# The local attention's exponential read from PSUM with the negated maximum as its bias, one instruction a head

## The chip, the cores and the metric

The kernel runs on one core of one Trainium2 chip. The metric is the device time of one execution in microseconds (us); lower is better. Three runs of the kernel before took 3838.45, 3840.28 and 3841.61 us; the median is 3840.28 us.

The engines are named as in the profile: PE is TensorE's matrix multiplication and PEld its loading of weights, DVE is VectorE, ACT is ScalarE, POOL is GpSimd, SP is SyncE, which issues the DMAs. PSUM has eight banks of 128 x 512 float32.

## The reference, cut to what matters

The program is a small two-stage network over 16 batches of 512 tokens with 128 features. In its first stage a gated recurrence (256 states) is gated by a two-layer transformer with local attention; in its second, an attention over all tokens (16 heads) is gated by experts. The change is in the local attention, which both layers have, with 8 heads of 64 and windows of 64 tokens:

```python
sim = jnp.einsum('bhwid,bhwjd->bhwij', bq, bk)
...
mask = (i < j) | (i > j + WINDOW) | (j == -1)
sim = jnp.where(mask, -jnp.finfo(sim.dtype).max, sim)
attn = jax.nn.softmax(sim, axis=-1)
out = jnp.einsum('bhwij,bhwjd->bhwid', attn, bv)
```

The softmax is computed as exp(sim - max), and the sum over the keys comes out of the product with the values, whose operand has a column of ones.

## The kernel before, in words

**The flows.** The work of one batch is cut into steps, and the steps belong to flows: `pre` (load and norm), `gru` (the gated recurrence), `attn0` and `attn1` (the local attention of the two layers), `post0` and `post1` (their feed-forward parts), `glob` (the attention over all tokens) and `expert`, which runs once. Four lanes hold them: lane a is attn0, post0, attn1 of batch b; lane s is post1 of batch b-1, gru of b, pre of b+1; lane g is the global attention of batches b-2 and b-1; lane x is the experts.

**What sets the order.** Each engine runs its own fixed sequence, once for each of 18 or so turns of a loop over the batches. The strings of `ORDER` (line 268) say from which lane the next step is taken: "a3g" is one step of lane a, then three of lane g. `merged` (line 281) reads them. Nothing is scheduled at run time. An engine waits on semaphores (`need`, line 314) for the step of another engine that it depends on, and what stands behind a waiting instruction waits too.

**The local attention.** A layer has a projection stage and a score stage. In the projection stage, for each of four tiles of 128 tokens (t = 0 to 3), PE computes q, k and v; ACT copies and squares q and k (L933, L936); DVE sums the squares (L1186) and multiplies by the rotary tables (`rot`: L1196, L1198, L1199); POOL adds the two products (L1385); DVE computes the inverse norms in three short instructions (`rot2`: L1207, L1209, L1211); POOL multiplies by them (L1390); PE turns q and k (`tq`, `tk`: L668) and ACT copies them to `qT` and `kT` (L956).

The score stage has eight units, one for each tile and each half of the heads, u = 2t + par. A unit covers 128 queries of four heads, and its scores fill one PSUM bank, `bank_a`: 128 queries x 4 heads x 128 keys. Its steps are

- `score`: PE writes the mask and the products into bank_a (line 678 on). DVE takes the maximum over the keys of each head (L1216), four columns in `stat`, and subtracts it (L1220), from bank_a into `prob[u % 2]` in SBUF;
- `prob`: ACT takes the exponential of `prob[u % 2]` in place, one instruction of 128 x 512 (L959);
- `pturn`: PE turns the probabilities in bank_b (L699), ACT copies them (L965);
- `pv`: PE multiplies by the values in bank_c; DVE takes the reciprocal of the sums (L1228) and scales (L1230);
- `oturn`, `wo`: every second unit, PE turns the output (L723), ACT copies it (L968), PE multiplies by the output weights, DVE adds to the residual (L1238).

There is one score bank. The next unit's `score` waits for the subtraction of the unit before it (line 674). The first projection of the next batch and the first matmul of `post0` wait for the last unit's subtraction (lines 651 and 740).

**What runs beside it.** The global attention has 64 score products a batch (`sim`, three banks of its own). DVE takes each one's negated maximum (L1292, `nmax`), ACT its exponential from PSUM with that column as bias and with the sum (L1022, followed by an ACTIVATION_READ_ACCUMULATOR), PE multiplies four of them by the scaled values (`av`, in o_bank), DVE takes a reciprocal (L1300) and POOL scales values by it (L1424). The recurrence's steps on DVE are L1134 to L1144 (`in_h`, `in_f`, `in_i`), L1148 to L1154, L1157 and L1158 (`g4`), and L1161, L1163 and L1165 (`g5`, the last one the scan).

## Time and profile before

| | |
|---|---|
| three timed runs | 3838.45, 3840.28, 3841.61 us |
| profiled execution, its own time | 3830.7 us |
| its span, first to last instruction | 3828.9 us |
| PE busy | 3102.7 us, 81% |
| DVE busy | 2714.3 us, 71% |
| ACT busy | 2401.6 us, 63% |
| POOL busy | 933.2 us, 24% |
| mean granted TensorE clock | 0.929 of full speed |

Busy time is the union of an engine's instructions, so neighbours that overlap are not counted twice; the busy time of a group of equal instructions is the sum of their durations. Start to start of two neighbours tells what an instruction costs its engine's queue, the duration tells when its result is there. The steady part repeats with a period of about 218.5 us a batch, so one period can be read for all, and the same place of a neighbouring batch lies 218.4 us away.

### The profile page before, as it was taken

The numbers are of one execution on the slowest core, as the hardware profiler recorded it, in microseconds if no ns is written. First come the engines' busy times: TensorE is split into PE (matmuls) and PEld (weight loads), VectorE is DVE, ScalarE is ACT, GpSimd is POOL, SyncE is SP. The second block draws the span as 40 slices with busy tenths as digits, with TensorE's granted clock in tenths as the row PEclk, the third lists the DMA queues.
The fourth block names the chain that finished last, engine by engine and source line by source line (L and its number), as shares of the span: only waits on it lengthen the run. The fifth ranks groups of instructions, "written<-read, shape, count | busy, mean of one in ns | idle before, by whom it ended". The sixth has DMA issues, their size and how long they took to land.

```text
span 3828.9 us, 55334 instructions
## 1 busy us (share of the span) xinstructions
PE 3102.7 (81%) x19984; PEld 1603.7 (42%) x20144; DVE 2714.3 (71%) x4829; ACT 2401.6 (63%) x5082; POOL 933.2 (24%) x685
## 2 busy tenths in 40 slices
PE   4668787888978787887978888897878789797786
PEld 2444443434444443444444344444444344444241
DVE  3476777868687886868687786868778686868432
ACT  2345666766666675766667676666667676666553
POOL 2021322222122322222132222213232221223100
PEclk7779898999999999999999899999989999999997
DMA  2001000010101001010100101010100101010200
GB/s 68 1 4 46 16 30 32 20 53 16 53 16 50 16 22 47 20 49 20 49 20 26 36 20 53 16 53 16 42 20 20 53 19 50 18 49 13 92 26 11
DMA packets 113451, 122.82 MB, mean 32 GB/s; under 512 B 13427, under 2 KB 86685, under 8 KB 113181
## 3 DMA queue, kind: packets, MB, share of 16 engines
q1 hardware_dynamic: 113180, 119.26, 9.7%
q8 instruction: 164, 2.69, 0.3%
q14 instruction: 107, 0.87, 0.1%
HBM read 64.70 MB, written 54.53 MB: 31 GB/s over the span
## 4 chain that ended last, share of the span: by engine, by line
PE 52%; DVE 26%; ACT 11%; issue 6%; POOL 5%; SPq 1%; DMA 0%; DVEq 0%; POOLq 0%; ACTq 0%
PE pb L573 29%; PE o_bank L573 12%; POOL scratch L1390 4%; DVE nmax L1292 4%; PE s L573 4%; PE pb L668 3%; PE pb L699 2%; DVE stat L1216 2%; ACT ex L1022 2%; DVE scratch L1220 2%; DVE scratch L1196 2%; DVE stat L1186 2%; PE pb L723 2%; DVE side L1158 1%; DVE scratch L1230 1%
## 5 line engine op out<-in xcount | busy, mean ns | idle before, releaser
L1022 ACT ACTIVATE ex<-s,nmax 128x512 f32<-128x512 f32 x1024 | 698.3, 686 | 279.7 <-DVE nmax L1292 257.1
L1292 DVE TENSOR_REDUCE nmax<-s 128x1 f32<-128x512 f32 x1024 | 676.2, 680 | 259.8 <-PE s L573 257.1
L573 PE MATMUL o_bank<-ex,vsc 128*64 128x512 f32 x2048 | 528.2, 638 | 84.6 <-POOL vsc L1424 84.2
L1424 POOL TENSOR_TENSOR vsc<-vrow,rinv 128x256 f32<-128x256 f32 x256 | 157.0, 613 | 1724.2 <-DVE rinv L1300 1724.2
L1385 POOL TENSOR_TENSOR scratch<-scratch 128x1024 f32<-128x1024 f32 x128 | 307.1, 2399 | 564.5 <-DVE scratch L1199 538.5
L573 PE MATMUL s<-qs,ks 96*128 96x512 bf16 x1024 | 345.2, 394 | 82.7 <-ACT ex L1022 82.7
L573 PE MATMUL pb<-wqkv,hsh 128*128 128x512 f32 x768 | 379.1, 622 | 33.8 <-DVE hsh L1179 26.1
L573 PE MATMUL pb<-kT,qT 64*64 64x64 f32 (+1 forms) x6144 | 330.8, 257 | 45.1 <-DVE scratch L1220 12.7
L959 ACT ACTIVATE scratch<-scratch 128x512 f32<-128x512 f32 x256 | 160.7, 628 | 321.1 <-DVE scratch L1220 321.0
L668 PE MATMUL pb<-const,scratch 128*128 128x128 f32 x1024 | 165.3, 308 | 242.2 <-POOL scratch L1390 242.2
L573 PEld LDWEIGHTS pb<-kT,qT 64*64 64x64 f32 x6144 | 282.9, 144 | 98.4 <-issue 98.4
L1390 POOL TENSOR_TENSOR scratch<-scratch,stat 128x1024 f32<-128x1024 f32 x128 | 258.1, 2017 | 191.6 <-DVE stat L1211 191.6
L573 PEld LDWEIGHTS o_bank<-ex,vsc 128*64 128x64 f32 x2048 | 133.3, 141 | 354.5 <-issue 249.2
L1216 DVE TENSOR_REDUCE stat<-pb 128x4 f32<-128x512 f32 x256 | 176.0, 687 | 136.1 <-PE pb L573 134.3
L668 PEld LDWEIGHTS pb<-const,scratch 128*128 128x128 f32 x1024 | 134.0, 160 | 320.0 <-issue 207.1
L573 PEld LDWEIGHTS s<-qs,ks 96*128 96x128 bf16 x1024 | 86.1, 98 | 382.5 <-issue 218.8
L573 PE MATMUL pb<-cent,w 128*128 128x512 f32 (+1 forms) x384 | 198.3, 627 | 42.6 <-ACT mlp_h L979 34.6
L573 PEld LDWEIGHTS pb<-wqkv,hsh 128*128 128x128 f32 x768 | 143.7, 197 | 204.1 <-issue 114.6
L956 ACT ACTIVATE qT<-pb 128x512 f32<-128x512 f32 x128 | 76.5, 598 | 220.1 <-PE pb L668 219.9
L933 ACT ACTIVATE scratch<-pb 128x512 f32<-128x512 f32 x256 | 151.9, 593 | 98.9 <-PE pb L573 97.1
L1022 ACT ACTIVATION_READ_ACCUMULATOR ex<-s,nmax 128x1 f32 x1024 | 208.2, 203 | 0.0
L573 PE MATMUL pb<-vb,scratch 128*64 128x65 f32 (+1 forms) x2176 | 192.8, 234 | 17.6 <-DVE scratch L1230 7.4
(190 smaller groups left out, 6108.9 us busy)
## 6 DMA issues: line engine op xcount, KB each, us to landing
parts_store<-side SPq DMA_DIRECT2D x64, 384.0 KB, 2.6
qs<-parts_store SPq DMA_DIRECT2D x128, 192.0 KB, 2.7
ks<-parts_store SPq DMA_DIRECT2D x128, 192.0 KB, 3.2
parts_store<-side SPq DMA_DIRECT2D x64, 256.0 KB, 2.9
parts_store<-side SPq DMA_DIRECT2D x64, 128.0 KB, 2.7
xin<-in_L_attn_x SPq DMA_DIRECT2D x16, 256.0 KB, 3.6
out<-o1T SPq DMA_DIRECT2D x16, 256.0 KB, 4.3
wqkv<-in_L_ffn_wqkv SPq DMA_DIRECT2D x1, 1536.0 KB
```

Source lines behind the costliest of these rows:

```text
L573: return pe.matmul(o, l, r, start=start, stop=stop, skip_group_check=True)
L668: last = pe.transpose(dst[:, P * r:P * r + P], l_q[:, INNER * k + P * r:INNER * k + P * r + P], ident)
L699: last = pe.transpose(bank_b[:, P * r:P * r + P], prob[u % 2][:, r, :], ident)
L723: last = pe.transpose(bank_b[:, P * r:P * r + P], o_row[:, P * r:P * r + P], ident)
L933: A(l_sq[:, INNER * k:INNER * (k + 1)], src, ACT.Square).then_inc(FA, 1)
L959: A(prob[s[1] % 2], prob[s[1] % 2], ACT.Exp).then_inc(FA, 1)
L1022: A(ex[:, w % 2, j, :], s_bank[(2 * NT + c) % SIMS][:], ACT.Exp, bias=nmax[:, c % 8:c % 8 + 1], accum_out=rsum[:, w % 2, j:j + 1]).then_in ...
L1216: V.tensor_reduce(top, sims, X, ALU.max).then_inc(FV, 1)
L1292: V.tensor_reduce(nmax[:, c % 8:c % 8 + 1], s_bank[(2 * NT + c) % SIMS][:], X, ALU.max, negate=True).then_inc(GV, 1)
L1385: G.tensor_tensor(l_q, l_c, l_s, ALU.add).then_inc(f.sem["pool"], 1)
L1390: G.tensor_tensor(q, q, stat[:, 96:112].unsqueeze(2).broadcast_to([P, 2 * HEADS, DH]), ALU.mult)\
L1424: G.tensor_tensor(vsc[:, w % 2].rearrange("p (m a) d -> p m a d", a=2), vrow[:, m:m + 2, 2 * V1 * p:2 * V1 * (p + 1)].rearrange("p m (a d) ...
```

## The change

DVE's maximum is written negated (`negate=True`), and its subtraction is dropped: the mark `sub` goes, and every wait for it becomes a wait for `prob`. The step `prob` on ACT now reads bank_a and writes `prob[u % 2]`. The bias of an ACT instruction is one value a partition, and the four heads have four maxima, so the exponential is four instructions of 128 x 128, each with its column of `stat`. The wait for the turn of unit u - 2, which frees `prob[u % 2]`, moves from DVE to ACT. Bank_a is now freed by the last of the four exponentials. The strings of ORDER are new for all four engines; a line of PE's stands here for them.

```diff
--- before.py
+++ after.py
@@ -188,7 +188,7 @@
     "rot2": {"dve": ["n1", "n2", "inv"], "pool": ["q"]},
     "tq": {"pe": ["t"], "act": ["t"]},
     "tk": {"pe": ["t"], "act": ["t"]},
-    "score": {"pe": ["s"], "dve": ["max", "sub"]},
+    "score": {"pe": ["s"], "dve": ["max"]},
     "prob": {"act": ["p"]},
     "pturn": {"pe": ["t"], "act": ["t"]},
     "pv": {"pe": ["o"], "dve": ["d", "o"]},
@@ -266,15 +266,14 @@
 ORDER = {
-    "pe": ("ga5g2asag2a4gsg5aga2gas3ag3s2a3gsas3gs3a3g3a2g5a2gagsg2ags3g2a2g3agsa2g2as3asg4ag3asa2ga2ga4xg3x4ga2"
...
+    "pe": ("ga4gag2as2a5gsg5ag2asg2as2ga2s3g2asas3gs2ag2a3g3ag3agags2a2gasga2gag2a2g3a3gas2as2agas2ag3asagxg2xa5"
...
@@ -648,7 +647,7 @@
                     elif t:
                         need(pe, f, "act", b, (kind, 0), "c")
                     elif kind == "q":
-                        need(pe, attn[1], "dve", b - 1, ("score", 2 * NT - 1), "sub")
+                        need(pe, attn[1], "act", b - 1, ("prob", 2 * NT - 1), "p")
                         need(pe, f, "dve", b, ("shift",), "h")
                     else:
                         need(pe, attn[1], "act", b - 1, ("oturn", NT - 1), "t")
@@ -671,7 +670,7 @@
                 elif kind == "score":
                     t, par = s[1] // 2, s[1] % 2
                     if s[1]:
-                        need(pe, f, "dve", b, ("score", s[1] - 1), "sub")
+                        need(pe, f, "act", b, ("prob", s[1] - 1), "p")
                     else:
                         need(pe, f, "act", b, ("tq", NT - 2), "t")
                     need(pe, f, "act", b, ("tk", t), "t")
@@ -737,7 +736,7 @@
                         need(pe, f, "pool", b, ("silu3",), "x")
                     else:
                         if l == 0:
-                            need(pe, attn[0], "dve", b, ("score", 2 * NT - 1), "sub")
+                            need(pe, attn[0], "act", b, ("prob", 2 * NT - 1), "p")
                         elif b == B - 1:
                             need(pe, gru, "act", b, ("out",), "o")
                         else:
@@ -955,8 +954,14 @@
                         dst, src = kT[:, :, WIN + P * t:WIN + P * t + P], bank_b if t < NT - 1 else bank_c
                     A(dst, src.rearrange("p (r n) -> p r n", r=PAIRS), ACT.Copy).then_inc(FA, 1)
                 elif kind == "prob":
-                    need(act, f, "dve", b, ("score", s[1]), "sub")
-                    A(prob[s[1] % 2], prob[s[1] % 2], ACT.Exp).then_inc(FA, 1)
+                    u = s[1]
+                    if u >= 2:
+                        need(act, f, "pe", b, ("pturn", u - 2), "t")
+                    need(act, f, "dve", b, ("score", u), "max")
+                    for r in range(PAIRS):
+                        last = A(prob[u % 2][:, r, :], bank_a[:, P * r:P * r + P], ACT.Exp,
+                                 bias=stat[:, 64 + 4 * (u % 2) + r:65 + 4 * (u % 2) + r])
+                    last.then_inc(FA, 1)
                 elif kind == "pturn":
                     u = s[1]
                     need(act, f, "pe", b, s, "t")
@@ -1213,11 +1218,7 @@
                     u = s[1]
                     need(dve, f, "pe", b, s, "s")
                     sims, top = bank_a.rearrange("p (h n) -> p h n", n=P), stat[:, 64 + 4 * (u % 2):68 + 4 * (u % 2)]
-                    V.tensor_reduce(top, sims, X, ALU.max).then_inc(FV, 1)
-                    if u >= 2:
-                        need(dve, f, "pe", b, ("pturn", u - 2), "t")
-                    need(dve, f, "dve", b, s, "max")
-                    V.tensor_tensor(prob[u % 2], sims, top.unsqueeze(2).broadcast_to([P, PAIRS, P]), ALU.subtract).then_inc(FV, 1)
+                    V.tensor_reduce(top, sims, X, ALU.max, negate=True).then_inc(FV, 1)
                 elif kind == "pv":
                     t, par = s[1] // 2, s[1] % 2
                     need(dve, f, "pe", b, s, "o")
```

The order of DVE in the second layer, from the end of the last tile's rotary products to unit 1's maximum. L1157 and L1158 are `g4`, L1161, L1163 and L1165 are `g5`, L1216 and L1220 the score unit's maximum and subtraction, L1207 to L1211 `rot2`. Before:

```order
L1199 TENSOR_TENSOR scratch<-scratch,tab 128x16x32
L1157 TENSOR_TENSOR side<-side 128x512
L1158 TENSOR_TENSOR side<-side 128x512
L1292 TENSOR_REDUCE nmax<-s 128x1
L1216 TENSOR_REDUCE stat<-pb 128x4
L1220 TENSOR_TENSOR scratch<-pb,stat 128x512
L1207 TENSOR_TENSOR stat<-stat 128x16
L1209 TENSOR_TENSOR stat<-stat 128x16
L1211 SCALAR_TENSOR_TENSOR stat<-stat 128x16
L1161 TENSOR_TENSOR side<-side 128x512
```

After, where L1204 is the old L1199, L1293 the old L1292, L1221 the old L1216, L1212 to L1216 the old L1207 to L1211, and L1162, L1163 and L1166 the old L1157, L1158 and L1161:

```order
L1204 TENSOR_TENSOR scratch<-scratch,tab 128x16x32
L1293 TENSOR_REDUCE nmax<-s 128x1 x3
L1301 RECIPROCAL rinv<-rsum 128x4
L1293 TENSOR_REDUCE nmax<-s 128x1
L1221 TENSOR_REDUCE stat<-pb 128x4
L1212 TENSOR_TENSOR stat<-stat 128x16
L1214 TENSOR_TENSOR stat<-stat 128x16
L1216 SCALAR_TENSOR_TENSOR stat<-stat 128x16
L1293 TENSOR_REDUCE nmax<-s 128x1
L1162 TENSOR_TENSOR side<-side 128x512
L1163 TENSOR_TENSOR side<-side 128x512
L1166 TENSOR_TENSOR side<-side 128x512
```

`g4` has moved from in front of the three short instructions to behind them, together with `g5`, and maxima of the global attention have moved in front.

The order of PE at the same place, from the end of unit 0's scores to the start of unit 1's. L668 is the turn of q and k of the last tile, `s<-qs,ks` a global score product, `pb<-masks,identb` the start of a unit's scores. Before:

```order
L573 MATMUL pb<-kT,qT 64x128
L573 MATMUL s<-qs,ks 128x512
L668 MATMUL pb<-const,scratch 128x128 x8
L573 MATMUL pb<-masks,identb 128x512
L573 MATMUL pb<-kT,qT 64x64 x2
```

After, with every line number one lower:

```order
L572 MATMUL pb<-kT,qT 64x128
L572 MATMUL s<-qs,ks 128x512 x2
L572 MATMUL o_bank<-ex,vsc 64x512 x4
L572 MATMUL s<-qs,ks 128x512 x3
L667 MATMUL pb<-const,scratch 128x128 x8
L572 MATMUL s<-qs,ks 128x512
L572 MATMUL pb<-xn,gru_w 128x512
L572 MATMUL pb<-masks,identb 128x512
```

Five global score products and a value product now stand in front of the turn instead of one score product, and one more and a recurrence input behind it.

## Rows read from the trace of the kernel before

**Rows 1.** The core: its span and mean granted clock.

```profile
core 0: 3828.9 us, clock 0.929
```

**Rows 2.** One period: us; busy PE, PEld, DVE, ACT, POOL; granted clock; DMA share; GB/s.

```profile
1610.50:1829.00 218.50, 183.02 (x1228) 94.19 (x1237) 167.53 (x298) 147.05 (x315) 58.24 (x43) 0.96 0.10 32
```

**Rows 3.** First layer's score stage, second layer's projections, second layer's burst.

```profile
1837.00:1885.00 48.00, 46.30 (x431) 27.22 (x434) 32.11 (x63) 30.36 (x68) 6.02 (x8) 1.00 0.10 34
1936.00:1947.00 11.00, 7.47 (x23) 2.36 (x22) 9.43 (x15) 9.40 (x20) 6.55 (x5) 0.84 0.06 23
1961.50:1991.30 29.80, 26.65 (x304) 17.63 (x309) 23.36 (x44) 17.25 (x35) 4.96 (x5) 0.94 0.05 15
```

**Rows 4.** The page: the chain that ended last, by engine.

```profile
PE 52%; DVE 26%; ACT 11%; issue 6%; POOL 5%; SPq 1%; DMA 0%; DVEq 0%; POOLq 0%; ACTq 0%
```

**Rows 5.** Groups by line and shape: busy us, mean ns | idle before, releaser.

```profile
L1022 ACT ACTIVATE ex<-s,nmax 128x512 f32<-128x512 f32 x1024 | 698.3, 686 | 279.7 <-DVE nmax L1292 257.1 <-DVE rinv L1300 22.1
L1220 DVE TENSOR_TENSOR scratch<-pb,stat 128x512 f32<-128x512 f32 x256 | 177.1, 692 | 22.1
L959 ACT ACTIVATE scratch<-scratch 128x512 f32<-128x512 f32 x256 | 160.7, 628 | 321.1 <-DVE scratch L1220 321.0
```

**Rows 6.** Timeline, first layer's score units: start us, us, engine, line [idle before].

```profile
1842.47 0.69 DVE L1216 TENSOR_REDUCE stat<-pb 128x4 f32<-128x512 f32 x1
1845.62 0.68 DVE L1216 TENSOR_REDUCE stat<-pb 128x4 f32<-128x512 f32 x1
1846.41 0.69 DVE L1220 TENSOR_TENSOR scratch<-pb,stat 128x512 f32<-128x512 f32 x1
...
1848.69 0.69 DVE L1216 TENSOR_REDUCE stat<-pb 128x4 f32<-128x512 f32 x1 [0.39 <-PE pb L573]
...
1847.13 0.63 ACT L959 ACTIVATE scratch<-scratch 128x512 f32<-128x512 f32 x1 [1.35 <-DVE scratch L1220]
```

**Rows 7.** Timeline of ACT: instructions that follow each other without a wait.

```profile
1921.36 0.69 ACT L1022 ACTIVATE ex<-s,nmax 128x512 f32<-128x512 f32 x1
1921.93 0.21 ACT L1022 ACTIVATION_READ_ACCUMULATOR ex<-s,nmax 128x1 f32 x1
...
1927.21 0.22 ACT L946 ACTIVATE stat<-stat 128x16 f32<-128x16 f32 x1
1927.46 0.31 ACT L948 ACTIVATE stat<-stat,cols 128x16 f32<-128x16 f32 x1
1927.67 0.58 ACT L933 ACTIVATE scratch<-pb 128x512 f32<-128x512 f32 x1
```

**Rows 8.** Timeline of DVE, POOL and PE at the second layer's hinge.

```profile
1948.82 0.68 DVE L1157 TENSOR_TENSOR side<-side 128x512 f32<-128x512 f32 x1
1949.42 2.83 DVE L1158 TENSOR_TENSOR side<-side 128x512 f32<-128x512 f32 x1
1952.17 0.68 DVE L1292 TENSOR_REDUCE nmax<-s 128x1 f32<-128x512 f32 x1
...
1955.31 2.27 DVE L1163 TENSOR_TENSOR side<-side 128x512 f32<-128x512 f32 x1
...
1948.98 2.72 POOL L1385 TENSOR_TENSOR scratch<-scratch 128x1024 f32<-128x1024 f32 x1 [2.90 <-DVE scratch L1199]
1954.81 2.22 POOL L1390 TENSOR_TENSOR scratch<-scratch,stat 128x1024 f32<-128x1024 f32 x1 [3.12 <-DVE stat L1211]
...
1957.17 1.94 PE L668 MATMUL pb<-const,scratch 128*128 128x128 f32 x8 [7.12 <-POOL scratch L1390]
```

**Rows 9.** Timeline of DVE in the second layer's burst.

```profile
1961.54 0.69 DVE L1216 TENSOR_REDUCE stat<-pb 128x4 f32<-128x512 f32 x1 [1.12 <-PE pb L573]
...
1986.64 0.68 DVE L1158 TENSOR_TENSOR side<-side 128x512 f32<-128x512 f32 x1
...
1991.22 0.68 DVE L1216 TENSOR_REDUCE stat<-pb 128x4 f32<-128x512 f32 x1
```

**Rows 10.** The stretch of the lower clock; columns as in the second group.

```profile
1951.50:1965.20 13.70, 7.67 (x48) 5.47 (x51) 10.93 (x16) 3.61 (x7) 2.42 (x2) 0.50 0.00 0
```

More of the change, by code:

```diff
@@ L268 @@
 ORDER = {
[L269 to L277 removed]
+    "pe": ("ga4gag2as2a5gsg5ag2asg2as2ga2s3g2asas3gs2ag2a3g3ag3agags2a2gasga2gag2a2g3a3gas2as2agas2ag3asagxg2xa5"
+           "x2gxagx3gxg4a2g2a2gagxgs6asgs4g5a4g5xagaxax2a3g2axa4gxg4xg2x2ags5as2as11aga2g2ag3asxg2as2gaxs16xg3xg"
+           "xa11xsag5xa3ga"),
+    "act": ("2ga3g4agagsa2gs4as2g4as3ags2g2s4a6g3asaga2g2asg2ag2agsga2s4gagagagagasg2s2asg2a2sa2sa2gxg2a6g4a4g3ag"
+            "3a2g4a3gx3ag2agags2a2gs3a3gxgasg3ag9a2gs2as2asa2g2agsg3xagsagsg2x2gx2sagx2g"),
+    "dve": ("a3gsx3gag2agsgaga3g2a2sa2gagagasgsgasa4g2sags2g2a2gas2ags2ga2gsg2aga3gas2gasags2a2sasg2a2s2as4x3ag3a"
+            "3g2ags2g2as2agsa4g2as2g2a3gxs3x2a5g2ag2sagsg2asasas4as2g2a4xsgas3a5g16xas2gaga5xg2sgxgax"),
+    "pool": ("2g3ag2ag3a2g2s5g3agasag2agsa2s3g"),
 }
```

8 lines of the change are left out of this document (removed).

## The prediction

> **What bounds the kernel now.** The core's span is 3828.9 us [rows 1]; the profiled execution took 3830.7 us, 1.8 us around the span, and the three timed runs have a median of 3840.28 us, 9.6 us above it. I make the sum against 3830.7 and add the 9.6 at the end.
>
> I read the busy time by stretch first. The program repeats once a batch, and a period of 218.5 us has PE busy for 183 us, DVE 168, ACT 147 and POOL 58 [rows 2]. None is full, so I asked where each one is. In the first layer's eight score units (48 us) PE is busy for 46.3 us: this stage is PE's. In the second layer's burst, from the max of unit 1 to the max of unit 7 (29.8 us), PE has 26.65 and DVE 23.36: two engines take turns. In 11 us of that layer's projections, shortly ahead of the burst, PE has only 7.5 while DVE has 9.4 [rows 3]. The chain that ended last says the same over the whole run: PE 52%, DVE 26%, ACT 11% [rows 4]. So DVE time is worth something in the second layer and little in the first.
>
> **The change part by part. 1, DVE.** There are 256 score units (2 layers, 8 units, 16 batches). Each loses the subtraction L1220, 692 ns long [rows 5], and the wait for its own max: the max starts at 1845.62, the subtraction at 1846.41, the next max can start at 1848.69 [rows 6]. From the max's start to the end of the subtraction that is 0.79 + 0.69 = 1.48 us of DVE's queue; a max alone takes 0.69. Neighbours overlap by some 0.1 us, so I count 0.70 us saved a unit, 11.2 us of the 168 in a period.
>
> **2, ACT.** One exponential of 128x512 without a bias column (L959, 628 ns [rows 5]) becomes four of 128x128 from PSUM with one. The trace of before has no such shape, so I bound it. The global attention's exponential, 128x512 from PSUM with a bias column, takes 686 ns [rows 5] and its follower starts 0.57 us after it; one of 16 columns from SBUF with a bias column (L948) takes 0.31 us and its follower starts 0.21 to 0.22 us after it [rows 7]. The slope between a 16-column and a 512-column instruction is (628 - 220) / 496 = 0.83 ns a column (L946 takes 0.22 us for 16 columns [rows 7], L959 628 ns for 512). So 128 columns from PSUM: 686 - 384 x 0.83 = 366 ns, follower after 570 - 320 = 250 ns. From SBUF: 0.31 + 112 x 0.83 ns = 0.40 us, follower after 0.31 us. Four then last 3 x 0.25 + 0.37 = 1.12 us, at most 3 x 0.31 + 0.40 = 1.33. If the bias were free while columns count alone, it would be the 0.63 of now. I take 1.12, the row with the same source and the same kind of bias. ACT's queue holds 1.0 us a unit instead of 0.52, 7.7 us more a period on an engine that has 147 of 218.5.
>
> The Trainium skill, ScalarE: Activation LUTs, section What ACT_TABLE_LOAD costs, gives 280 ns + 0.833 ns a column for an instruction with a pointer bias and 93 ns of overlap between neighbours. As an estimate by that page four take 3 x 294 + 387 = 1.27 us, 0.15 us a unit more than by my row; on the at most eight tight handovers counted below that would add 1.2 us a period.
>
> **3, the score bank is held longer.** Now bank_a is free when the subtraction ends, 1.48 us after the max starts [rows 6]. After the change it is free when the fourth exponential ends: max 0.69, 0.03 to ACT (the subtraction ends at 1847.10, L959 starts at 1847.13 [rows 6]), then 1.12: 1.84 us. So a tight handover is 0.36 us later (0.57 by the upper bound; below nothing if the exponentials took 0.63). The tight cadence is 3.07 us now, 1845.62 to 1848.69 [rows 6], and becomes 3.43. The probabilities themselves are ready sooner: 0.79 + 0.69 + 0.03 + 0.63 = 2.14 us after the max now, 1.84 then.
>
> In the first layer PE is the bound and PE's work there is unchanged. Two of its handovers are tight, 3.15 us from 1842.47 and 3.07 from 1845.62 [rows 6], so I charge 2 x 0.36 = 0.7 us a period, with nothing gained.
>
> **4, the new order at the second layer's hinge.** This is where I expect most. Now PE stands idle for 7.12 us before the last turn of q (L668, 1957.17), until POOL's L1390 that starts at 1954.81. L1390 waits for DVE, which first does L1157 and L1158 of the gated recurrence (from 1948.82; L1158 alone takes 2.83 us beside POOL's L1385, against 0.68 where POOL is idle, 1986.64), one global max, the max and the subtraction of unit 0, and only then the three short instructions [rows 8, 9]. In the new order L1157 and L1158 stand behind those three, and two global maxima come in front. From the end of L1199 to the three: minus 3.35 us (1948.82 to 1952.17, where the global max starts), minus 0.70 for the subtraction, plus 2 x 0.6 for the maxima, plus 0.1 for a reciprocal: 2.75 us earlier, so the turn of q starts at 1954.4 instead of 1957.2. PE gets five score products and one value product of the global attention in front of that turn (0.3 to 0.4 each and 1.9 us), so the 7.1 us of idleness nearly fill up. But unit 1's max now has L1157 to L1165 in front of it. After the three at 1951.8 stand one global max, 0.6, and a recurrence of 0.6 + 2.8 + 0.7 + 0.7 + 1.3 (its L1163 took 2.27 beside POOL [rows 8] and should now miss it): the earliest max of unit 1 is 1958.5. On PE's side it waits for the turns, a recurrence input and a score, 4.4 + 1.9 us at today's pace: 1960.7. Now it is 1961.54 [rows 9]. The gain lies between 0.8 and 3 us; I take 1.5.
>
> **5, the burst behind it.** From unit 1's max to unit 7's it is 29.7 us now (1961.54 to 1991.22 [rows 9]). Of PE's work 1.9 us of value product and four score products of 0.35 have moved ahead: 3.3 us. Of DVE's, six subtractions (4.2 us) and three maxima (1.8) are gone and two recurrence inputs (1.3) come in: 4.7 us. The longer hold costs between nothing and 6 x 0.36 = 2.2; other work of PE stands between most pairs of scores, so I take 0.8. With the smaller of the two gains that is 3.3 - 0.8 = 2.5 us. If every handover is bound by the bank, the floor is 6 x 3.43 = 20.6 us, still below PE's 23.
>
> **Sum:** +0.7 - 1.5 - 2.5 = -3.3 us a period, 16 periods: -53 us. 3830.7 - 53 + 9.6 = 3787 us. Its own range, from the bounds of parts 4 and 5 (-2 to -5 a period): 3760 to 3808.
>
> **Rivals.**
> A, the clock comes back as well. For the 13.7 us from 1951.5 the granted clock is 0.50, the lower level (1.2 GHz) [rows 10], and this follows PE's idleness at the hinge. If the fill of part 4 keeps it at 2.4 GHz, the 7.67 us of PE work in that window [rows 10] halve: 3.8 us more a period, -7.1 in all, 3726 us. For it: the fill stands exactly in the gap. Against it: PE would still wait for the turns, and DVE holds unit 1 back.
>
> B, slower: the exponentials come late in ACT's queue, and the bank with them. Today a late exponential holds nothing but its own transposition, since the bank is DVE's to free. Place: the seven handovers of the first layer, where PE has 1.7 us of slack in 48 [rows 3]. Price: one global exponential ahead on ACT, 0.57 us, and the 0.36, 0.93 x 7 = 6.5 us, less the 4.0 of the second layer: +2.5 a period, 3840 + 40 = 3880 us. It decides from 4.0 / 7 = 0.57 us a handover, that is, once the exponentials start 0.21 us late on average. For it: ACT starts L959 0.03 us behind DVE only where it is idle [rows 6]. Against it: ACT has 147 of 218.5.
>
> C, no change: another loop through PE sets the period. PE's 183 us a period are not touched by any edit, and what the second layer gains is waited away in front of the next stage: 3840 us.
>
> **Chances.** Forecast 0.44, A 0.18, B 0.25, C 0.13. A measurement of this kernel tells 0.2%, some 8 us, from no change. Faster 0.62, same 0.13, slower 0.25. The range leaves out the outer half of B and little of A: 3722 to 3868 us.
>
> **What would show it.** Right: DVE busy for 157 us a period, ACT for about 155; the four exponentials 0.25 us apart and 0.37 long; the wait before the last turn of q in the second layer under 4 us; unit 1 to unit 7 in 26 to 28 us; the first layer's 48 us within 1 us. A: no half clock in the burst. B: PE's waits for the exponentials sum to over 5 us a period in the first layer. Wrong in part 2: an exponential over 0.40 us. The forecast falls if the first layer grows by more than the second one gives back, or if a longer half clock appears.

## The result, and the profile after

The changed kernel takes 3906.98 us (3904.78 to 3908.12, four runs) against 3839.36 us before: the ratio is 1.0176, 95% interval [1.0159, 1.0194]. It is slower by 68 us, 4.2 us a period; the forecast was 53 us faster. The profiled execution has this core:

```profile
core 0: 3904.8 us, clock 0.920
```

The period seen from one first maximum of the first layer to the next, in four stages: the first layer's units 0 to 7; from its last maximum to unit 1's in the second layer; the second layer's burst (unit 1 to 7); and the rest. Columns as in [rows 2]. Before:

```profile
1831.10:1871.40 40.30, 38.39 (x373) 22.59 (x378) 32.71 (x65) 28.62 (x67) 7.99 (x9) 1.00 0.05 15
1871.40:1961.50 90.10, 69.13 (x306) 32.31 (x307) 62.94 (x100) 53.54 (x108) 26.09 (x16) 0.93 0.16 54
1961.50:1991.20 29.70, 26.55 (x303) 17.53 (x308) 23.27 (x43) 17.25 (x35) 4.96 (x5) 0.94 0.05 15
1991.20:2049.40 58.20, 48.87 (x249) 21.72 (x249) 48.45 (x90) 47.42 (x105) 19.04 (x13) 1.00 0.06 19
```

After: the period, then the same four stages, and the burst of a later batch.

```profile
1883.10:2108.40 225.30, 192.46 (x1237) 97.53 (x1238) 157.20 (x282) 155.35 (x362) 57.31 (x42) 0.94 0.10 31
1883.10:1924.70 41.60, 38.96 (x375) 22.18 (x376) 28.19 (x58) 30.91 (x84) 8.53 (x9) 1.00 0.04 11
1924.70:2015.50 90.80, 73.68 (x321) 32.79 (x320) 59.96 (x102) 57.94 (x123) 25.39 (x16) 0.94 0.17 55
2015.50:2049.70 34.20, 29.92 (x294) 20.49 (x295) 19.69 (x35) 17.92 (x46) 4.38 (x4) 0.75 0.05 13
2049.70:2108.40 58.70, 49.90 (x250) 22.07 (x251) 49.35 (x90) 48.58 (x109) 19.01 (x13) 1.00 0.07 19
...
2691.50:2721.00 29.50, 24.41 (x294) 17.15 (x295) 19.13 (x35) 17.92 (x46) 4.38 (x4) 0.94 0.05 14
```

This period is 225.3 us against 218.3: +1.3 in the first layer, +0.7 up to unit 1, +4.5 in the burst, +0.5 behind it. DVE and ACT, at 157.20 and 155.35 us, are busy just as forecast ([rows 2] had 168 and 147). The burst shows two things. At a mean clock of 0.75 it takes 34.2 us; two of eleven batches, with the clock that [rows 3] had (0.94), take 29.5 and 30.0. So at the old clock nothing is gained where 2.5 us were forecast, and in the other nine the lower clock adds 4.7. (Averaged over batches 4 to 14, counted from 0, the period is 219.7 us before and 224.3 after, since two of before's take 224.4 with 37.5 us at half clock.)

The chain that ended last, for [rows 4], has passed from DVE to ACT:

```profile
PE 53%; DVE 20%; ACT 17%; issue 5%; POOL 4%; SPq 1%; DMA 0%; POOLq 0%; DVEq 0%; ACTq 0%
```

The groups and one tight handover in the first layer, for [rows 5] and [rows 6]:

```profile
L962 ACT ACTIVATE scratch<-pb,stat 128x128 f32<-128x128 f32 x1024 | 291.9, 370 | 329.1 <-DVE stat L1221 321.8
```

```profile
1895.53 0.69 DVE L1221 TENSOR_REDUCE stat<-pb 128x4 f32<-128x512 f32 x1 [0.17 <-PE pb L572]
...
1896.32 1.14 ACT L962 ACTIVATE scratch<-pb,stat 128x128 f32<-128x128 f32 x4
...
1897.51 0.39 PE L572 MATMUL pb<-masks,identb 128*128 128x512 bf16 x1 [0.49 <-ACT scratch L962]
```

Each exponential lasts 0.37 us, four take 1.14, and the next starts (1.14 - 0.37) / 3 = 0.26 us behind the last: the 0.37, 1.12 and 0.25 of part 2. The next scores start 1.98 us after the maximum. Before they could start 1.53 us after it, when their weights were loaded behind the subtraction (the maximum of [rows 6] starts at 1845.62):

```profile
1847.15 0.10 PEld L573 LDWEIGHTS pb<-masks,identb 128*128 128x128 bf16 x1 [0.57 <-DVE scratch L1220]
```

So a handover is 0.45 us longer where 0.36 were forecast; most of the missing 0.09 is ACT's start, 0.79 us after the maximum's start instead of 0.72.

The hinge, for [rows 8]: PE, POOL, DVE and ACT.

```profile
1997.73 1.12 PE L572 MATMUL o_bank<-ex,vsc 128*64 128x512 f32 x2 [4.22 <-POOL vsc L1425]
...
2007.25 1.94 PE L572 MATMUL o_bank<-ex,vsc 128*64 128x512 f32 x8 [1.41 <-POOL vsc L1425]
...
2011.15 1.06 PE L667 MATMUL pb<-const,scratch 128*128 128x128 f32 x8 [1.21 <-POOL scratch L1391]
...
1995.98 1.60 POOL L1425 TENSOR_TENSOR vsc<-vrow,rinv 128x256 f32<-128x256 f32 x1
...
2003.70 2.35 POOL L1386 TENSOR_TENSOR scratch<-scratch 128x1024 f32<-128x1024 f32 x1 [3.02 <-PE pb L667]
...
2002.36 0.68 DVE L1204 TENSOR_TENSOR scratch<-scratch,tab 128x512 f32<-128x512 f32 x1
...
2005.66 0.69 DVE L1293 TENSOR_REDUCE nmax<-s 128x1 f32<-128x512 f32 x1 [1.43 <-PE s L572]
...
2008.38 0.17 DVE L1212 TENSOR_TENSOR stat<-stat 128x16 f32<-128x16 f32 x1 [0.76 <-ACT stat L947]
...
2007.79 0.21 ACT L945 ACTIVATE stat<-stat 128x16 f32<-128x16 f32 x1
```

The 7.12 us before the turn of q are now 1.21, but 4.22 and 1.41 us stand in front of two value products: 6.84 us in all. The first of these two products stood at the same place before and waited there too, 2.17 us, so that its wait grew by 2.05:

```profile
1940.75 3.21 PE L573 MATMUL o_bank<-ex,vsc 128*64 128x512 f32 x8 [2.17 <-POOL vsc L1424]
```

In the changed kernel it waits for POOL's L1425, which stands behind a rotary sum and then takes 1.60 us. And the three short instructions of DVE come no sooner after the last rotary product than they did: 6.02 us (2002.36 to 2008.38), against 5.88 before (1948.21 to 1954.09). DVE waits there 1.43 us for a score product that PE has not issued and 0.76 us for ACT's L947, which in the new order stands behind four global exponentials.

Unit 1's scores then wait another 0.69 us for unit 0's exponentials. These start 5.86 us after their maximum (2006.93), behind ACT's two copies of the turned q and k:

```profile
2012.79 1.15 ACT L962 ACTIVATE scratch<-pb,stat 128x128 f32<-128x128 f32 x4
...
2013.99 0.39 PE L572 MATMUL pb<-masks,identb 128*128 128x512 bf16 x1 [0.69 <-ACT scratch L962]
```

PE's waits in the burst at the clock of 0.94 (us in total, times, longest), before (1961.5 to 1991.2) and after (2691.5 to 2721.0):

```profile
PE pb L573 <- DVE scratch L1220: 0.4, 1, 0.4
PE pb L723 <- ACT scratch L965: 0.2, 1, 0.2
```

```profile
PE pb L572 <- ACT scratch L962: 2.2, 2, 1.4
...
PE pb L722 <- ACT scratch L970: 1.3, 1, 1.3
```

PE's work there fell from 26.55 to 24.41 us, its idle time rose from 29.7 - 26.55 = 3.15 to 29.5 - 24.41 = 5.09. The bank costs 1.8 us more, and the copy of the turned probabilities (L970, the old L965), which now stands behind four exponentials on ACT, 1.1 more; a wait for DVE's scaling grew by 0.6, and small ones of 1.0 in all are gone.

The same sums over the whole run, before and then after:

```profile
PE pb L668 <- POOL scratch L1390: 242.2, 98, 8.1
PE o_bank L573 <- POOL vsc L1424: 84.2, 61, 6.0
PE s L573 <- ACT ex L1022: 82.7, 73, 2.5
...
PE pb L573 <- DVE scratch L1220: 20.6, 36, 1.2
```

```profile
PE o_bank L572 <- POOL vsc L1425: 153.0, 89, 4.5
PE s L572 <- ACT ex L1027: 108.4, 91, 2.5
PE pb L667 <- POOL scratch L1391: 81.7, 83, 7.0
PE pb L572 <- ACT scratch L962: 60.9, 72, 1.8
```

The hinge's own wait lost 160 us; the value products' got 69 back, the global scores' 26 and the score bank's 40 (60.9 for 20.6).

### The profile page after: what moved, and what is told of

The parts are those of the page before. It is cut to its first block, busy times and chain, and to the rows that moved or that the text cites. A ratio compares the mean times of both kernels' runs of the same rounds, so it can differ in the third digit from the quotient of the medians.

```text
span 3904.8 us, 56006 instructions
## 1 busy us (share of the span) xinstructions
PE 3220.5 (82%) x20144; PEld 1637.3 (42%) x20144; DVE 2544.2 (65%) x4573; ACT 2536.7 (65%) x5850; POOL 922.2 (24%) x685
## 4 chain that ended last, share of the span: by engine, by line
PE 53%; DVE 20%; ACT 17%; issue 5%; POOL 4%; SPq 1%; DMA 0%; POOLq 0%; DVEq 0%; ACTq 0%
PE pb L572 32%; PE o_bank L572 12%; ACT ex L1027 4%; PE s L572 3%; ACT scratch L962 3%; PE pb L698 3%; DVE nmax L1293 3%; DVE scratch L1201 2%; DVE stat L1191 2%; POOL scratch L1391 2%; DVE stat L1221 1%; PE pb L667 1%; POOL vsc L1425 1%; PE pb L722 1%; POOL scratch L1386 1%
## 5 line engine op out<-in xcount | busy, mean ns | idle before, releaser
L1293 DVE TENSOR_REDUCE nmax<-s 128x1 f32<-128x512 f32 x1024 | 676.6, 679 | 320.0 <-PE s L572 317.2
L572 PE MATMUL o_bank<-ex,vsc 128*64 128x512 f32 x2048 | 546.0, 657 | 155.2 <-POOL vsc L1425 153.0
L1425 POOL TENSOR_TENSOR vsc<-vrow,rinv 128x256 f32<-128x256 f32 x256 | 171.5, 670 | 1623.2 <-DVE rinv L1301 1623.1
L962 ACT ACTIVATE scratch<-pb,stat 128x128 f32<-128x128 f32 x1024 | 291.9, 370 | 329.1 <-DVE stat L1221 321.8
L572 PE MATMUL pb<-wqkv,hsh 128*128 128x512 f32 x768 | 378.2, 624 | 35.0 <-DVE hsh L1184 27.5
L572 PE MATMUL pb<-kT,qT 64*64 64x64 f32 (+1 forms) x6144 | 346.1, 265 | 0.0
L572 PEld LDWEIGHTS pb<-kT,qT 64*64 64x64 f32 x6144 | 296.8, 150 | 93.2 <-issue 93.2
L1221 DVE TENSOR_REDUCE stat<-pb 128x4 f32<-128x512 f32 x256 | 176.5, 690 | 216.3 <-PE pb L572 215.0
L932 ACT ACTIVATE scratch<-pb 128x512 f32<-128x512 f32 x256 | 152.4, 595 | 100.7 <-PE pb L572 100.6
L667 PE MATMUL pb<-const,scratch 128*128 128x128 f32 x1024 | 149.3, 290 | 81.7 <-POOL scratch L1391 81.7
L572 PE MATMUL pb<-vb,scratch 128*64 128x65 f32 (+1 forms) x2176 | 205.7, 243 | 9.9 <-DVE x L1239 6.5
L973 ACT ACTIVATE scratch<-pb 128x512 f32<-128x512 f32 x128 | 76.8, 600 | 209.9 <-PE pb L722 209.9
L572 PEld LDWEIGHTS pb<-vb,scratch 128*64 128x64 f32 (+1 forms) x2176 | 170.4, 152 | 95.0 <-issue 52.2
```

The source lines that it names most:

```text
L572: return pe.matmul(o, l, r, start=start, stop=stop, skip_group_check=True)
L667: last = pe.transpose(dst[:, P * r:P * r + P], l_q[:, INNER * k + P * r:INNER * k + P * r + P], ident)
L932: A(l_sq[:, INNER * k:INNER * (k + 1)], src, ACT.Square).then_inc(FA, 1)
L962: last = A(prob[u % 2][:, r, :], bank_a[:, P * r:P * r + P], ACT.Exp, bias=stat[:, 64 + 4 * (u % 2) + r:65 + 4 * (u % 2) + r])
L1221: V.tensor_reduce(top, sims, X, ALU.max, negate=True).then_inc(FV, 1)
L1293: V.tensor_reduce(nmax[:, c % 8:c % 8 + 1], s_bank[(2 * NT + c) % SIMS][:], X, ALU.max, negate=True).then_inc(GV, 1)
```

## The experiments

Times are medians, and the ratio is to the kernel before on the same chip (3837 to 3839.5 us), with its 95% interval. Stage lengths and half-clock times are means over batches 4 to 14, from maximum to maximum. The clock's price stands apart in a few places: for each kernel I added up PE's busy time inside the stretches of the lower clock (1.2 GHz for 2.4) and halved it, and call what is left of the period the rest. It takes PE to be the bound in those stretches, so it is an upper bound.

| kernel | period | clock | rest |
|---|---|---|---|
| before | 219.7 | 7.3 | 212.4 |
| after | 224.3 | 11.1 | 213.2 |
| old order, four exponentials | 239.2 | 18.3 | 221.0 |
| old order, hold alone | 236.7 | 16.3 | 220.4 |
| new order, first head's maximum | 215.7 | 3.9 | 211.8 |
| the same, ACT's queue filled | 218.5 | 7.1 | 211.4 |
| new order, joint maximum | 216.9 | 6.1 | 210.8 |

**1. The two halves of the change apart.** The body of after with the order of before, and the reverse.

```diff
 ORDER = {...}          # e1_exp_old_order: after.py with the four strings of before.py
 ORDER = {...}          # e2_new_order_only: before.py with the four strings of after.py
```

> The changed exponential with the ORDER strings of the kernel before. Clock theory (the loss of about 67 us comes from the lower clock in the second layer's burst, which the new order brings about by taking PE's filler out of the burst): the granted clock keeps the pattern of before, about 17 us at the lower level a period, and the time is 3835 to 3860 us. Hold theory (the loss comes from the score bank, held about 0.44 us longer at each tight handover, whatever the order): 3880 to 3920 us, with handovers of 1.97 us after the max.

> The kernel before with the ORDER strings of the changed one; DVE's subtraction and the single exponential stay. Clock theory in its form that the order alone removes the filler: 3870 to 3920 us, with 25 us or more at the lower clock a period. Hold theory: the order is harmless and its shorter hinge pays, 3800 to 3845 us.

Measured: 4115.77 us, 1.0730 [1.0701, 1.0759], and 3909.98 us, 1.0192 [1.0166, 1.0217]. The four corners:

| | order of before | order of after |
|---|---|---|
| subtraction on DVE | 3837 | 3910 |
| four exponentials from the bank | 4116 | 3907 |

They don't add up. In the old order the exponentials cost 279 us; the new order alone costs 73, and within it the body is worth nothing (-3, which the intervals don't tell from 0). So the order is needed by the new body and is dear by itself.

**2. The longer hold alone.** DVE still subtracts, but the next scores wait for the exponential.

```diff
-                        need(pe, f, "dve", b, ("score", s[1] - 1), "sub")
+                        need(pe, f, "act", b, ("prob", s[1] - 1), "p")
```

> The kernel before, with one wait changed: the next unit's scores wait for the exponential instead of the subtraction, so the bank is held some 0.65 us longer and nothing else moves. Hold theory: with about 8 tight handovers a period that is at least 4 to 5 us a period, 3905 to 3925 us. Clock theory: only where the extra gap tips the clock is it more than 2 us a period; without a tip 3845 to 3875 us.

> The new order with the subtraction kept and the bank freed by the exponential (the longer hold alone, in the new order; the same edit in the old order cost 248 us). If the new order was laid out for the exponential to free the bank (ACT's exponentials start early in it): 3925 to 3990 us. If the hold costs the same in any order: 4130 to 4170 us.

Measured: 4085.03 us, 1.0651 [1.0626, 1.0675], in the old order; 3937.97 us, 1.0284 [1.0246, 1.0321], in the new one. One wait moved costs 248 us in the old order and 28 in the new. So most of the old order's loss comes when ACT and not DVE releases the bank, already with one exponential a unit: PE's waits for the bank are 156.5 us with the moved wait and 159.8 in the kernel of the first experiment, against 20.6 before, and the first layer's 40.3 us became 50.8 and 55.5.

```profile
PE pb L573 <- ACT scratch L959: 156.5, 107, 2.6
```

```profile
PE pb L573 <- ACT scratch L963: 159.8, 93, 3.1
```

**3. One exponential instead of four.** The first head's maximum serves as bias for all four heads.

```diff
-                    for r in range(PAIRS):
-                        last = A(prob[u % 2][:, r, :], bank_a[:, P * r:P * r + P], ACT.Exp,
-                                 bias=stat[:, 64 + 4 * (u % 2) + r:65 + 4 * (u % 2) + r])
-                    last.then_inc(FA, 1)
+                    A(prob[u % 2], bank_a.rearrange("p (h n) -> p h n", n=P), ACT.Exp,
+                      bias=stat[:, 64 + 4 * (u % 2):65 + 4 * (u % 2)]).then_inc(FA, 1)
```

> The changed exponential as one instruction of 128x512 with one head's maximum as the bias of all four heads (the other three heads' probabilities are therefore wrong), in the order of before. The bank is held 0.72 + 0.69 = 1.41 us, less than the 1.54 of before, and DVE loses its subtraction. Hold theory: faster than before by 1 to 3 us a period, 3790 to 3825 us. Clock theory: the pattern of the clock as before or better, 3780 to 3840 us. If it is no faster than before, DVE's subtraction was worth nothing in that order.

> The changed kernel in its own order, with the exponential as one instruction of 128x512 whose bias is one head's maximum (the other three heads' probabilities are wrong). ACT's queue is relieved by 0.4 us a unit and the bank is free 0.4 us sooner after the max. Handover theory (the burst of the second layer is set by the chain score, max, exponential, next score, so DVE's and PE's relief is worth nothing): 4 to 5 handovers a layer shorten by 0.4 us, 3 to 4 us a period, 3845 to 3865 us. If the chain is not in the handovers: 3890 to 3910 us.

(Both texts call the other three heads' probabilities wrong. That was mistaken: a row's exponentials and their sum carry the same factor, whatever was subtracted, and the division takes it out as long as nothing overflows.)

Measured: 4001.95 us, 1.0432 [1.0408, 1.0457], in the old order; 3767.09 us, 0.9799 [0.9766, 0.9833], in the new one. In the old order both theories had a time near or below that of before, and both missed: although DVE has lost its subtraction, the kernel is 165 us slower than before, and PE still waits 131.3 us for the bank, with 50.2 us for the first layer. The split adds 114 us there.

```profile
PE pb L573 <- ACT scratch L962: 131.3, 94, 2.7
```

In the new order the split into four costs 140 us. Read from the kernel with the new order and the old body (3910), dropping the subtraction and taking the exponential from the bank is worth 143 us, and the split takes 140 of them back. By the table the split's 8.6 us a period are 7.2 of clock and 1.4 of rest, and the rest is nearly the first layer's 1.2 (41.5 us against 40.3).

**4. The bank or ACT's queue?** One exponential, and behind it, when the bank has been let go, two of one column that keep ACT busy.

```diff
+                    for i in range(2):
+                        c = 52 + 4 * l + 2 * (u % 2) + i
+                        A(cols[:, c:c + 1], norm_bias, ACT.Exp, bias=norm_bias)
```

> The kernel with one exponential 128x512 per unit in the changed order (3767 us, the first head's maximum serves all four), and behind each exponential, after it has let the bank go, a wait that is long met and two exponentials of one column into cells that nobody reads: some 0.22 us each, so that ScalarE is occupied about as long per unit as with the four exponentials (1.12 against 0.69 us), while the bank is released as early as with one. Theory 'the longer hold of the bank is the price of the split': the time stays near the kernel with one exponential, 3767 to 3795 us, and the handover from maximum to next scores stays 0.4 us shorter than in the changed kernel. Rival 'ScalarE's own time is the price' (the copies of the turned probabilities queue behind the exponentials): 3870 to 3905 us, near the changed kernel's 3907.

Measured: 3826.27 us, 0.9972 [0.9960, 0.9985], between the two theories. ACT is held 0.69 us and then 0.47 more:

```profile
1850.55 0.69 ACT L961 ACTIVATE scratch<-pb,stat 128x512 f32<-128x512 f32 x1 [0.34 <-DVE stat L1224]
1851.14 0.47 ACT L967 ACTIVATE cols<-cols 128x1 f32<-128x1 f32 x2
1851.51 0.58 ACT L973 ACTIVATE scratch<-pb 128x512 f32<-128x512 f32 x1
```

ACT's longer queue costs 59 of the 140 us, and neither theory had that. The first layer stays at 40.4 us and a burst without half clock takes 27.9 us instead of 27.5; but half clock falls in more batches (15.5 us a period against 8.7), and in the table the whole difference is clock. The remaining 81 us belong to the longer hold, by subtraction and not by a run of its own.

**5. Why the old order loses so much.** First the four steps `prob` 1, 2, 5 and 6 of the first layer moved forward in ACT's row, because they started up to 5.5 us after their maximum; then, on PE instead, work moved in front of two score units.

```diff
 ACT (e10_early_prob):  prob 1, 2, 5, 6 of attn0 moved ahead of the steps they stood behind
 PE  (e15_pe_moves):   +av.11, sim 12.2, sim 12.3    ahead of attn0's score.1
                       +av.14                        ahead of attn0's score.6
```

> The changed exponential in the order of before, which cost 279 us more than before, with four steps moved in ACT's order of the first layer alone: the exponentials of units 1, 2, 5 and 6 stand earlier, ahead of the gate's silu1 and silu2, of three global exponentials and of the first query projection. Late-exponential theory (rival B of the prediction: in the old order the exponential starts up to 5.5 us after its max, and now it holds the bank): the first layer's score stage falls from 55.7 us by 5 us or more, 3990 to 4050 us. If the length of the hold alone counts, not its start: 4090 us or more.

> The exponentials from the bank in the order of before (4116 us, first layer's units 0 to 7 in 55.5 us), and on TensorE three steps of the first layer's stretch moved: the global attention's value product 11 and two of its score groups ahead of unit 1's scores, value product 14 ahead of unit 6's scores. VectorE's, ScalarE's and GpSimd's orders are those of before. Theory 'the scores stand too early in TensorE's row, and everything behind them waits for the bank': TensorE has work for the 2 to 3 us in which it now stands before units 1 and 6, the stretch falls to 49 to 52 us and the time to 4020 to 4080 us. Rival 'what fails in that order is the other engines' turn, not TensorE's': the moved steps were not late, the stretch stays within 1 us of 55.5 and the time within 15 of 4116.

Measured: 4096.12 us, 1.0653 [1.0609, 1.0696], and 4061.93 us, 1.0583 [1.0560, 1.0605], against 4115.77 unmoved. In the first, the exponentials of those units start 0.79 us or less after their maximum and the first layer still takes 55.1 us. The bank's waits over the run fell from 159.8 to 119.6 us, but the global scores' waits for ACT rose from 79.1 to 105.5: the steps that were passed over came late instead. Late exponentials alone were therefore not what held it; an order of ACT without either delay was not tried. In the second it falls from 55.5 to 50.7 us, PE's waits for the bank from 159.8 to 102.2, and the rest of the period from 221.0 to 215.7. So PE's row is a part of it, 54 of the 279 us: a score unit that stands too early there stops all work behind it. The row before unit 1's scores in the unmoved kernel:

```profile
1979.75 0.61 PE L573 MATMUL pb<-masks,identb 128*128 128x512 bf16 x1 [3.11 <-ACT scratch L963]
```

The other 10 us of that stage are not accounted for by a run, nor is it known which places in the rows make up the rest of the 279.

**6. The hinge in the kernel before.** `g4` (L1157, L1158) moved behind the last `rot2` of the second layer, nothing else; then the same with 12 bf16 matmuls of 128x512 ahead of the turn of q, whose results are overwritten; and 24 of them in the kernel before as it was.

```diff
 DVE:  -L1157, L1158    ahead of L1207, L1209, L1211 (second layer, tile 3)
       +L1157, L1158    behind them
+                    if l and t == NT - 1 and not k:
+                        for _ in range(12):      # 24 in e6_filler_before
+                            mm(dst, identb[:], masks[:, 0, :, :].rearrange("p h n -> p (h n)"))
```

> The kernel before with one move in DVE's order: the recurrence's L1157 and L1158 stand behind the three short instructions of the last tile instead of in front of them, which is the prediction's part 4 alone. The prediction's reasoning: the turn of q starts some 3.3 us earlier and unit 1's max 1 to 3 us earlier, 3790 to 3825 us. If the recurrence then holds unit 1's max back by as much: 3835 to 3850 us.

> The kernel before with the recurrence's L1157 and L1158 moved behind the three short instructions, which gave 3816 us, and 12 bf16 products of the mask as filler in PE's gap of 4 us before the last turn of q in the second layer. In the run without filler the batches alternate between 216 and 221 us with 13.7 and 27.3 us at the lower clock. Clock theory: all batches near 216 us or less, 3770 to 3800 us. If the dips only wander to the next stage, as in the changed kernel with filler: 3805 to 3825 us.

> The kernel before, with 24 bf16 products of the mask in the 7.12 us for which PE stands idle before the last turn of q in the second layer; their results are overwritten. Clock theory: the 13.7 us at the lower clock behind that gap go or shrink, 3 to 4 us a period less, 3775 to 3800 us. If PE's pace in that stretch does not set the time: 3830 to 3850 us.

Measured: 3816.01 us, 0.9948 [0.9933, 0.9964]; 3786.68 us, 0.9847 [0.9805, 0.9889]; and 3829.12 us, 0.9985 [0.9975, 0.9995]. The hinge's move is worth 21 us alone. Its batches come in two kinds: six of eleven take 215.9 to 218.1 us with 13.7 to 23.9 at half clock, and five take 221.0 with 27.3. In the best, unit 1's maximum comes 0.9 us earlier and the burst is 1.5 us shorter (28.2). Filling PE's gap behind the move brings another 29 us, with half clock down from 20.8 to 9.6 us a period (read from its fastest execution, 3773 us; the four go up to 3795). Without the move the filler brings 8 us: half clock falls from 21.4 to 15.5 us, but in seven of eleven batches the turn of q starts 0.7 to 2.0 us later after unit 0's maximum than before.

**7. The clock in the changed kernel.** Fillers of the same kind in the second layer's burst (after: five ahead of unit 2's scores, five and three ahead of the first two output turns and projections; joint maximum: three and three at the first output turn and projection), and one value product moved back behind unit 0's value product.

```diff
+                        if l and s[1] == 2:                      # e5_filler_after, and at two more places
+                            need(pe, f, "act", b, ("tk", NT - 1), "t")
+                            for _ in range(5):
+                                mm(bank_c, identb[:], masks[:, 0, :, :].rearrange("p h n -> p (h n)"))
 PE (e12_av3_back):    -av.3 ahead of attn1's pv.0
                       +av.3 behind it
```

> The changed kernel with idle PE time filled in the second layer's burst: five bf16 products of the mask (0.22 us each at the upper clock) before unit 2's scores, and five and three before the turn of the output and the output product of tiles 0 and 1. Their results are overwritten. Clock theory, in the form left after the first runs (in the new order the lower clock in this burst costs some 6 us a period: batches whose burst runs at the upper level take 219.3 us against 225.3): less than 20 us at the lower clock a period and 3815 to 3875 us. If the clock is only a follower and the waits set the time: 3905 to 3930 us, the filler adding a little.

> The changed kernel with one move in PE's order: the value product of global head 3 (1.9 us) goes back from the gap before the last turn of q into the burst, behind unit 0's value product, where it stood before the change. Clock theory: the burst keeps the upper clock in most batches, 29.5 to 31 us instead of 34.2, 3830 to 3875 us. If the dips come anyway: 3895 to 3920 us.

> The kernel with one joint maximum and one exponential, and in the second layer three matmuls 128x512 in bf16 ahead of the first turn of the attention's output and three ahead of the first output projection, whose results are overwritten: work that keeps TensorE from standing still there, where the granted clock falls in the time after the second layer's burst (8.7 us at half clock per period with one exponential). Theory 'the clock's fall costs there': the half-clock time falls to 4 us or less and 1 to 2 us per period come back, 3735 to 3755 us. Rival 'the fillers cost what they save', as in the changed kernel, where fillers took the half-clock time from 24.5 to 13.7 us and left the time at 3904: 3760 to 3785 us.

Measured: 3903.95 us, 1.0175 [1.0158, 1.0191]; 3922.78 us, 1.0205 [1.0169, 1.0241]; and 3848.99 us, 1.0027 [1.0016, 1.0038], which is 72 us above its own base. In the first, no half clock is left in the burst, which falls from 33.4 to 31.7 us, but the stage behind it grows by 1.7. In the third, six fillers a period make the base worse: its burst, 27.5 us in the base's undisturbed batches, is 31.7 at a clock of 0.89, and the stage ahead of it is 2.4 us longer.

```profile
1885.90:1977.00 91.10, 75.24 (x320) 33.38 (x320) 59.26 (x103) 57.09 (x117) 25.38 (x16) 0.93 0.17 55
1977.00:2008.70 31.70, 25.59 (x295) 18.35 (x301) 19.86 (x35) 15.22 (x28) 5.35 (x4) 0.89 0.04 13
```

In the first the clock's price falls from 11.1 to 6.2 us and the rest rises from 213.2 to 217.4, about the fillers' own time (21 of 0.22 us, 4.6 us); in the third the price rises from 6.1 to 9.1 although PE is busier. In the second, the burst takes 33.8 us and 27.3 us of the period are at half clock. None gained. What the clock costs can be read; where it falls could not be steered by these fillers.

**8. One joint maximum, one exponential.** A softmax row may be shifted by any number, so four heads can share one maximum.

```diff
-                    V.tensor_reduce(top, sims, X, ALU.max, negate=True).then_inc(FV, 1)
+                    V.tensor_reduce(top[:, 0:1], bank_a, X, ALU.max, negate=True).then_inc(FV, 1)
```

with ACT's single instruction of the third experiment.

> The changed kernel with one maximum per unit over all four heads' scores (a reduction 128x512 to 128x1, negated) and one exponential 128x512 with it as bias. A softmax may be shifted by any number, so the four heads may share one maximum; the work per element on VectorE is what it was. Theory 'the split holds the bank': VectorE's reduction of the same 512 columns takes the same 0.72 us as now, the handover from one unit's scores to the next is that of the kernel with one exponential and the first head's maximum, and so is the time, 3767 us, within 10. Rival 'the maximum's result comes sooner or later with one group instead of four': each of 15 handovers moves by 0.1 us, 16 x 1.5 = 24 us, 3743 or 3791 us.

Measured: 3776.76 us, 0.9841 [0.9820, 0.9862]. This version beats both kernels, before by 62 us and the change by 130. No exponential exceeds one; a head whose largest score lies some 87 below the joint maximum would underflow in float32, which is the condition on the data under which it may be used. Its handover and two bursts, of neighbouring batches:

```profile
1814.50 0.68 DVE L1218 TENSOR_REDUCE stat<-pb 128x1 f32<-128x512 f32 x1
...
1815.28 0.69 ACT L961 ACTIVATE scratch<-pb,stat 128x512 f32<-128x512 f32 x1
...
1817.56 0.69 DVE L1218 TENSOR_REDUCE stat<-pb 128x1 f32<-128x512 f32 x1 [0.75 <-PE pb L572]
```

```profile
1931.40:1958.90 27.50, 22.02 (x290) 16.03 (x295) 19.76 (x36) 15.11 (x28) 4.78 (x4) 1.00 0.05 16
...
2146.60:2177.20 30.60, 26.14 (x290) 18.67 (x294) 19.50 (x35) 15.22 (x28) 4.38 (x4) 0.83 0.05 14
```

From maximum to maximum 3.06 us, against 3.52 with four exponentials (1895.53 to 1899.05) and 3.07 before. Six of eleven batches have the slower burst, against two of eleven with the first head's maximum: four times 3.1 us, which is about the 10 us between the two kernels (3767 and 3777).

## Why the prediction was wrong

**Part 1, DVE,** held: 157 us a period. With ACT answering in one instruction, the new body was worth 143 us in the new order.

**Part 2, ACT,** held: 1.14 us for 1.12. The upper bound of 1.33 and the 1.27 estimated by the Trainium skill (ScalarE: Activation LUTs, What ACT_TABLE_LOAD costs) were both too high here.

**Part 3, the hold,** held nearly in size, 0.45 us for 0.36. The first layer grew by 1.3 us where 0.7 were charged: three of its handovers are tight and not two, 1 to 2, 2 to 3 and 5 to 6, each 3.5 us from maximum to maximum, and 0.25, 0.46 and 0.27 us longer than with one exponential.

**Part 4, the hinge, is the first step that failed.** I moved DVE's three short instructions forward by what left DVE's queue in front of them, and took all else as ready. What they need from ACT (L947), and the score products that the maxima in front of them need from PE, had been moved back in those engines' rows, and they came 6.02 us after the rotary product, as before. PE's wait before the turn did shrink, as forecast, but the value product a step earlier waited 4.22 us instead of 2.17, because its scale had queued on DVE and POOL, and a second value product waited 1.41. With the subtraction kept and the new order alone, the same three waits are 4.21, 1.41 and 1.21 us: they come from the order and not from the exponentials. Alone in the order of before, the move of `g4` brought 21 us (experiment 6), near the 16 x 1.5 = 24 forecast, though more of it in the burst than up to unit 1's maximum; so it is the rest of the new order that took it back.

Of the -1.5 us to unit 1's maximum the period above has +0.7. From the first layer's last maximum to it, PE's idle time fell from 90.10 - 69.13 = 20.97 us to 90.80 - 73.68 = 17.12, but its busy time rose by 4.55: the idleness was filled with moved work, and no time came out. The clock explains little of this. One place in this stretch is slower by 1.7 us, six matmuls of `post0` that take 4.44 us in the changed kernel and 2.74 in the one with one exponential, as in the kernel before (at 1907.99):

```profile
1961.69 4.44 PE L572 MATMUL pb<-mlp_h,w 128*128 128x512 f32 x6
```

```profile
1878.18 2.74 PE L572 MATMUL pb<-mlp_h,w 128*128 128x512 f32 x6
```

But over the whole of it half clock lasted 13.5 us before and 10.2 after, and its price, by the upper bound above, is 3.9 and 4.3 us. My 1.5 also leaned on a quicker PE: at the old pace my own figure for PE's side gave 0.8.

**Part 5, the burst, is the term that decides,** and it failed three times over. Of 3.3 us of PE's work that I moved ahead, 2.1 left the burst. For the hold I charged 0.8 us, because other work of PE stands between the scores; it cost 1.8, not because every handover was tight but because two were very tight (1.4 and 0.8 us of waiting). And I charged nothing for what queues behind the exponentials on ACT, PE's 1.1 us for the copy of the turned probabilities: I had called the longer ACT queue 7.7 us on an engine with 147 of 218.5, that is, by its share and not by who waits behind it. Together -2.1 and +1.9: nothing gained at the clock of [rows 3]. Then the clock, of which the sum had nothing: 17.1 us of the burst are at the lower level ((1 - 0.75) x 2 x 34.2), against 3.6 in [rows 3], and that makes the 4.7 us. Rival A had the clock come back because PE's longest gap was filled. The gap was filled and the clock fell further: what stood ahead of the burst's half clock were waits of 4.2, 1.4, 1.2, 0.7 and 1.4 us.

**The rivals.** B came nearest in sign and time (3880), and the place where it looked is where the old order lost; there PE's row made up a part of the loss, and ACT's row was not cleared. In the changed kernel the exponentials of units 1 to 6 in the first layer and 1 to 7 in the second start 0.73 to 0.81 us after the maximum, and PE waits 1.2 us a period for them in the first layer, where B's sign was over 5. So B's mechanism isn't what happened there; it shows in one place, the 0.69 us that unit 1's scores wait at the second layer's hinge for unit 0's late exponentials. C's loop through PE fell with the kernel that takes 3767.

**The balance,** a period, by the table's estimate: 3.8 of the 4.7 us are clock and 0.9 the rest (before rounding), and the rest is about the first layer's 1.3. With the clock's price taken out, this change would be a near-tie with a small loss; the direct price of the split is 1.4 us. Since the clock's price is an upper bound, so is its share.

**Not settled:** why the clock falls in one batch's burst and not in the next one's with the same order. The clock was changed only through waits and fillers, never by itself, so that the waits lower it is what fits these runs and not a thing shown apart.

## What to carry to other kernels

When a step hands a shared buffer on, price the edit by the time from the buffer's filling to its release, and then by who waits behind it on the engine that inherits the work; a share of busy time hides both. Where a per-group operand forces several instructions on the inheriting engine, look for a freedom of the algebra (here the softmax's shift) that makes the operand common: one instruction instead of four was 130 us. And read PE's granted clock beside every stage, since here the lower clock made up most of the loss (7.2 of the split's 8.6 us a period, by the estimate above). And when a step moves forward in a fixed order, look up each of its operands on its own engine's row: where they had moved back, here, the step came no sooner.

## What was unexpected of the hardware

- With the same instructions in the same order, the burst took 27.5 us at a clock of 1.00 and 30.6 at 0.83 in neighbouring batches. The burst of the changed kernel at 0.75 has no wait of PE over 1.4 us in it.
- An exponential of 128 columns from PSUM takes 370 ns, the one of 512 columns 687. ACT started on unit 1, where it waits for DVE alone, 0.72 to 0.73 us after the maximum's start, and on most later units, where it waits for PE's turn too, 0.79 after it.
- POOL's scaling of 128x256 takes 0.61 us, and in the changed kernel 1.60 in 15 of its 256 instances, once a batch, beside a two-operand DVE instruction of 128x1024 that takes 1.70 us (its L1157, the old L1152), as L1158 was slowed beside POOL in [rows 8]:

```profile
1995.41 1.70 DVE L1157 TENSOR_TENSOR side<-side 128x1024 f32<-128x1024 f32 x1
```
